# Dot products kept as three components through the edge loop of a graph convolution, and folded per node in the last stage

## The reference, cut to what matters

```
w = edge_query @ tp_weight                      # 224 weights an edge
out0 = w0 * es * sh_s                           # 64
out1 = (w1 * es)[:, :, None] * sh_v             # 64 x 3
out2 = 2**-0.5 * (w2a*sh_s) * ev + 0.5 * w2b * cross(ev, sh_v)      # 32 x 3
out3 = 3**-0.5 * w3 * sum(ev * sh_v, axis=-1)   # 32, the dot products
agg  = segment_sum([out0, out1, out2, out3], edge_dst)              # 384 a node
scal = [a0, a3] @ lin2_w0 / 96**0.5;  vec = [a1, a2] @ lin2_w1 / 96**0.5
x = layernorm(x + skip + [scal, vec] / 10)
```

## Time and profile before

| what | value |
|---|---|
| median of three runs | 7921.6 us (7917.41 to 7922.39) |
| profiled execution, its own time | 7914.6 us |
| its span, first to last instruction | 7912.8 us |
| busy over the span: PE, DVE, ACT, POOL | 89%, 96%, 66%, 68% |
| conv_edges, first L1345 to last L1280 | 5429.6 to 7837.2 us |
| conv_output, from there to the end | 75.6 us |

### The profile page before, as it was taken

How to read it: one execution, slowest core, us unless ns; L and a number is a source line. 1 busy time by engine, 2 the same in 40 slices (tenths; PEclk the granted TensorE clock), 3 DMA queues, 4 the chain that set the end, 5 groups by cost and what they waited for, 6 DMA issues and landing times. The chain is left out here.

```text
span 7912.8 us, 199441 instructions
## 1 busy us (share of the span) xinstructions
PE 7045.1 (89%) x48227; PEld 5905.9 (75%) x48227; DVE 7568.2 (96%) x18615; ACT 5259.2 (66%) x18286; POOL 5348.1 (68%) x5500
## 2 busy tenths in 40 slices
PE   6999999999999999999999859998888888888888
PEld 4888888888888888888888848875555555555556
DVE  4999999999999999999999889976999999999999
ACT  2666666666666666666666634435788788788786
POOL 2777777777777777777777436634777777777773
PEclk5999999999999999999999979977999999999999
DMA  3444444434434344343434337732333333333332
GB/s 105 107 109 109 106 107 106 107 106 106 107 105 107 106 107 106 106 108 105 107 106 107 89 128 260 257 117 69 94 93 91 90 91 90 91 91 90 91 91 59
DMA packets 815660, 856.41 MB, mean 108 GB/s; under 512 B 413920, under 2 KB 623200, under 8 KB 815072
## 3 DMA queue, kind: packets, MB, share of 16 engines
q0 software_dynamic: 241920, 413.20, 21.8%
q1 hardware_dynamic: 573088, 438.30, 18.1%
q10 hardware_dynamic: 576, 4.01, 0.1%
HBM read 706.51 MB, written 148.44 MB: 108 GB/s over the span
## 5 line engine op out<-in xcount | busy, mean ns | idle before, releaser
L1243 POOL DMA_INDIRECT agg<-tab_conv,ce_idx x1808 | 1708.7, 945 | 841.3 <-issue 621.8
L471 POOL DMA_INDIRECT ae_gdst<-tab_dst,ae_idx x1616 | 1683.9, 1042 | 528.0 <-issue 528.0
L468 POOL DMA_INDIRECT ae_gsrc<-tab_src,ae_idx x1616 | 1538.5, 952 | 674.4 <-issue 523.9
L1333 PE MATMUL psum<-ce_prod,ce_plain 128*128 128x384 f32 x3616 | 1539.7, 507 | 302.5 <-ACT ce_prod L1318 302.1
L1318 ACT ACTIVATE ce_prod<-ce_raw,ce_y 128x64 f32<-128x64 f32 x5424 | 1464.8, 333 | 0.0
L1316 ACT ACTIVATE ce_prod<-ce_raw,ce_y 128x160 f32<-128x160 f32 x1808 | 753.2, 417 | 488.8 <-DVE ce_raw L1264 488.8
L1335 PEld LDWEIGHTS psum<-ce_prod,ce_plain 128*128 128x128 f32 x3616 | 687.6, 190 | 479.6 <-issue 1.5
L713 ACT ACTIVATE ae_second_t<-psum 128x512 f32<-128x512 f32 x1212 | 732.2, 604 | 462.0 <-PE psum L623 456.1
L1333 PEld LDWEIGHTS psum<-ce_prod,ce_plain 128*128 128x128 f32 x3616 | 546.9, 191 | 449.5 <-DVE ce_plain L1294 276.2
L631 PE MATMUL psum<-pack_sb,ae_first_t 128*128 128x200 f32 x3232 | 850.1, 345 | 2.2 <-ACT ae_first_t L709 2.0
L641 PE MATMUL psum<-pack_sb,ae_second_t 128*128 128x96 f32 x3232 | 665.1, 288 | 129.1 <-ACT ae_second_t L713 126.7
(11 more groups left out here) (216 smaller groups left out, 19066.1 us busy)
## 6 DMA issues: line engine op xcount, KB each, us to landing
ag_val<-h_dram SPq DMA_DIRECT2D x452, 320.0 KB, 4.0
h_dram<-ae_hout SPq DMA_DIRECT2D x404, 320.0 KB
agg<-in_query SPq DMA_DIRECT2D x452, 128.0 KB
ae_rin<-in_rin SPq DMA_DIRECT2D x404, 128.0 KB
agg<-tab_conv,ce_idx POOLq DMA_INDIRECT x1808
ae_gsrc<-tab_src,ae_idx POOLq DMA_INDIRECT x1616
ae_gdst<-tab_dst,ae_idx POOLq DMA_INDIRECT x1616
ce_idx<-in_eidx SPq DMA_DIRECT2D x452, 4.0 KB
```

Source lines behind the costliest of these rows:

```text
L468: pool.indirect_dma_start(gsrc[t.slot4][:, k, :], None, g["tab_src"], bass.IndirectOffsetOnAxis(ap=idx[t.slot4][:, k:k + 1], axis=0))\
L471: pool.indirect_dma_start(gdst[t.slot4][:, k, :], None, g["tab_dst"], bass.IndirectOffsetOnAxis(ap=idx[t.slot4][:, 4 + k:5 + k], axis=0))\
L1243: pool.indirect_dma_start(node[t.slot8][:, k, :], None, g["tab_conv"], bass.IndirectOffsetOnAxis(ap=idx[t.slot8][:, k:k + 1], axis=0))\
L1333: pe.matmul(b_a[t.slot], plain[t.slot4][:, k, :], prod[t.slot][:, k, 96:480], start=(k == 0), stop=False, skip_group_check=True)
```

## The change

- `prod` is 544 columns wide for each k instead of 480, the block's sum `b_a` 448 instead of 384, `agg1` 448 a node. The three components of a dot product stay apart: columns 352 to 448 of a node hold 3 x 32.
- DVE: the sum over components (L1287) and the product of 128 elements (L1306) are gone. In L1287's place stands one product of 384 elements, weights times `diag`, straight into `prod`. L1303 is now the last of the step and raises `prod_done`. L1280 adds 448 columns.
- PE: L1333 has 448 columns. ACT writes the same sizes to other columns.
- conv_output: 14 additions at the head of DVE's stream fold the three components into one; PE's transposes wait for the fold of their seven blocks. One of the three products has 160 output columns (it had 64) and comes first.
- The table `yy` of the attention layer is allocated in an inner scope.

```diff
+AGG = 448
-        prod = [sb(f"prod{u}", [P, 4, 480]) for u in range(2)]
+        prod = [sb(f"prod{u}", [P, 4, V3 + AGG]) for u in range(2)]
...
-        b_a = [banks[4 + u][:, 0:384] for u in range(2)]
+        b_a = [banks[4 + u][:, 0:AGG] for u in range(2)]
...
-                        wait(dve, dot_done, t.n)
+                        wait(dve, prod_done, t.n)
                         dve.tensor_tensor(both[:, :, :, :, :].rearrange("p k d x c -> p k d (x c)"),
...
-                        dve.tensor_reduce(dot[:, :, :], diag[:, :, :, :].rearrange("p k x c -> p k c x"), AX, ALU.add).then_inc(dot_done, 1)
+                        wait(dve, summed, t.n - 1)
+                        dve.tensor_tensor(comps(prod[t.slot][:, :, 448:544]), b_w[t.slot][:, :, 192:WW].unsqueeze(2).to_broadcast(three),
+                                          diag, ALU.mult)
...
                         dve.wait_ge(cross_done, t.n + 1)
-                        wait(dve, summed, t.n - 1)
-                        dve.tensor_tensor(out[:, :, 192:480].rearrange("p k (x c) -> p k x c", x=3)[:, :, :, CS:96],
-                                          bank[:, :, 160:192].unsqueeze(2).to_broadcast(three), cross[:, :, :, :], ALU.mult)
-                        dve.wait_ge(dot_done, t.n + 1)
-                        dve.tensor_tensor(out[:, :, 160:192], bank[:, :, 192:WW], dot[:, :, :], ALU.mult).then_inc(prod_done, 1)
+                        dve.tensor_tensor(out[:, :, 160:448].rearrange("p k (x c) -> p k x c", x=3)[:, :, :, CS:96],
+                                          bank[:, :, 160:192].unsqueeze(2).to_broadcast(three), cross[:, :, :, :], ALU.mult)\
+                            .then_inc(prod_done, 1)
...
-                            pe.matmul(b_a[t.slot], plain[t.slot4][:, k, :], prod[t.slot][:, k, 96:480], start=(k == 0), stop=False,
+                            pe.matmul(b_a[t.slot], plain[t.slot4][:, k, :], prod[t.slot][:, k, 96:544], start=(k == 0), stop=False,
...
+                for c, (a, z) in enumerate(SEVENS):
+                    dot = agg[:, a:z, 352:384]
+                    dve.tensor_tensor(dot, dot, agg[:, a:z, 384:416], ALU.add).then_inc(halved, 1)
+                    dve.wait_ge(halved, c + 1)
+                    dve.tensor_tensor(dot, dot, agg[:, a:z, 416:448], ALU.add).then_inc(folded, 1)
...
+                        pe.wait_ge(folded, b // 7 + 1)
...
-                        pe.matmul(b_o[b % 4][:, 0:96], feat[b % 4][:, 0, :], w("l2a"), start=True, stop=False, skip_group_check=True)
-                        pe.matmul(b_o[b % 4][:, 64:128], feat[b % 4][:, 1, :], w("l2b"), start=False, stop=False, skip_group_check=True)
-                        pe.matmul(b_o[b % 4][:, 96:160], feat[b % 4][:, 2, :], w("l2c"), start=False, stop=True, skip_group_check=True)\
+                        pe.matmul(b_o[b % 4][:, 0:C], feat[b % 4][:, 2, :], w("l2c"), start=True, stop=False, skip_group_check=True)
+                        pe.matmul(b_o[b % 4][:, 0:96], feat[b % 4][:, 0, :], w("l2a"), start=False, stop=False, skip_group_check=True)
+                        pe.matmul(b_o[b % 4][:, 64:128], feat[b % 4][:, 1, :], w("l2b"), start=False, stop=True, skip_group_check=True)\
```

More of the change, by code:

```diff
@@ L54 @@
     ("ts1", 64, 128), ("tv1", 96, 192), ("tp", 128, 224),
[1 row of a table removed]
+    ("l2a", 128, 96), ("l2b", 128, 64), ("l2c", 128, C),
 ]
@@ L113, in gnn @@
         step_b = top.enter_context(nc.sbuf_tensor("step_b", [P, STEPS], I32))
-        yy = top.enter_context(nc.sbuf_tensor("yy", [P, 4 * SUPER], F32))
         psum = top.enter_context(nc.psum_tensor("psum", [P, 8, 512], F32))
         banks = [psum[:, i, :] for i in range(8)]
-        g = dict(psum=psum, pack=pack, nodes=nodes, block128=block128, step_s=step_s, step_b=step_b, banks=banks, yy=yy,
+        g = dict(psum=psum, pack=pack, nodes=nodes, block128=block128, step_s=step_s, step_b=step_b, banks=banks,
                  tab_src=tab_src, tab_dst=tab_dst, tab_conv=tab_conv, h_dram=h_dram, io=io)
@@ L123, in gnn @@
         g["w"] = w
-        attention_input(nc, g)
         with ExitStack() as mid:
@@ L128, in gnn @@
             with ExitStack() as upper:
+                g["yy"] = upper.enter_context(nc.sbuf_tensor("yy", [P, 4 * SUPER], F32))
+                attention_input(nc, g)
                 g["alpha"] = upper.enter_context(nc.sbuf_tensor("alpha", [P, SCANT, H], F32))
@@ L134, in gnn @@
                 attention_aggregate(nc, g)
-            g["agg1"] = mid.enter_context(nc.sbuf_tensor("agg1", [P, BLOCKS, 384], F32))
+            g["agg1"] = mid.enter_context(nc.sbuf_tensor("agg1", [P, BLOCKS, AGG], F32))
             attention_output(nc, g)
@@ L1208, in conv_edges @@
         diag, plus = both[:, :, 0, :, :], both[:, :, 1, :, :]
-        cross, dot = sb("cross", [P, 4, 3, CV]), sb("dot", [P, 4, CV])
+        cross = sb("cross", [P, 4, 3, CV])
         loaded, gathered = ([sem(f"{x}{u}") for u in range(8)] for x in ("loaded", "gathered"))
-        may_gather, iota_done, raw_done, outer_done, cross_done, plain_done, turned_y, dot_done, prod_done = (sem(x) for x in (
-            "may_gather", "iota_done", "raw_done", "outer_done", "cross_done", "plain_done", "turned_y", "dot_done", "prod_done"))
+        may_gather, iota_done, raw_done, outer_done, cross_done, plain_done, turned_y, prod_done = (sem(x) for x in (
+            "may_gather", "iota_done", "raw_done", "outer_done", "cross_done", "plain_done", "turned_y", "prod_done"))
         scaled, weights, summed, added = (sem(x) for x in ("scaled", "weights", "summed", "added"))
         b_w = [psum[:, 2 * u:2 * u + 2, :].rearrange("p b (k c) -> p (b k) c", k=2)[:, :, 0:WW] for u in range(2)]
-        b_a = [banks[4 + u][:, 0:384] for u in range(2)]
+        b_a = [banks[4 + u][:, 0:AGG] for u in range(2)]
         minus = banks[6][:, 0:384].rearrange("p (k x c) -> p k x c", k=4, x=3)
@@ L1317, in body @@
                         for x in range(3):
-                            ins = act.activation(prod[t.slot][:, k, 192 + 96 * x:256 + 96 * x], raw[t.slot][:, k, 160:WW], ACT.Identity,
+                            ins = act.activation(prod[t.slot][:, k, 160 + 96 * x:224 + 96 * x], raw[t.slot][:, k, 160:WW], ACT.Identity,
                                                  scale=y[t.slot8][:, k, x + 1:x + 2])
@@ L1332, in body @@
                         for k in range(4):
-                            pe.matmul(b_a[t.slot], plain[t.slot4][:, k, :], prod[t.slot][:, k, 96:480], start=(k == 0), stop=False,
+                            pe.matmul(b_a[t.slot], plain[t.slot4][:, k, :], prod[t.slot][:, k, 96:544], start=(k == 0), stop=False,
                                       skip_group_check=True)
-                            ins = pe.matmul(b_a[t.slot][:, 96:384].rearrange("p (x c) -> p x c", x=3)[:, :, CS:96],
+                            ins = pe.matmul(b_a[t.slot][:, 64:352].rearrange("p (x c) -> p x c", x=3)[:, :, CS:96],
                                             plain[t.slot4][:, k, :], prod[t.slot][:, k, 0:96].rearrange("p (x c) -> p x c", x=3),
@@ L1364, in conv_output @@
         turned, kept, mapped, added, rooted, stored = (sem(x) for x in ("turned", "kept", "mapped", "added", "rooted", "stored"))
+        halved, folded = sem("halved"), sem("folded")
         phase = [sem("phase0"), sem("phase1")]
@@ L1513, in lay_pack @@
     lin_s, lin_v = L1["lin2_w0"], L1["lin2_w1"]
-    W["l2a"][0:96, 0:64], W["l2a"][96:128, 64:96] = lin_s, lin_v[0:32]
-    W["l2b"][0:64, 0:32], W["l2b"][64:128, 32:64] = lin_v[32:96], lin_v[0:64]
-    W["l2c"][0:32, 0:32], W["l2c"][32:128, 32:64] = lin_v[64:96], lin_v
+    W["l2a"][0:64, 0:64], W["l2a"][64:128, 64:96] = lin_s[0:64], lin_v[0:64]
+    W["l2b"][0:32, 0:32], W["l2b"][32:128, 32:64] = lin_v[64:96], lin_v
+    W["l2c"][0:96, 128:160], W["l2c"][96:128, 0:64] = lin_v, lin_s[64:96]
     out = np.zeros((P, PACKW), np.float32)
```

## The result

The changed kernel takes 7954.1 us (median of 6 runs, 7951.5 to 7956.8), the kernel before 7917.9 us in the same comparison (6 runs, 7913.1 to 7922.4). The ratio is 1.0046, 95% interval 1.0033 to 1.0059. It is slower by 36 us; forecast were 58, and the range 7945 to 8012 holds it.

The account below looks back on a forecast made before the run. The prediction took DVE, at 5.296 us a step, as the bound, with the ring of engines 0.20 us in two steps behind. 54 us in conv_edges plus 4 in conv_output made 58, forecast 7980 us, range 7945 to 8012.

Parts of the forecast that it names:

- the ring of two steps: conv_edges: chain through DVE, ACT and PE from L1261 to L1261 two steps later, growing from 10.39 to 10.83 us.
- The sign that was expected: conv_edges: L1261 on DVE waits for PE's L1345 in nearly every step, 0.2 to 0.35 us.
- `prod_done` comes earlier, but PE's wait is for ACT, so nothing is gained there: conv_edges, PE's wait before the sums: the earlier semaphore gains nothing; ACT's end to PE's start stays 0.20 us.
- PE's end to L1262: conv_edges: joint from the end of PE's weights to DVE's first instruction of a step (L1261 before), 0.11 us.
- What returns every eight steps: conv_edges: 56 turns of the eight-step loop, up to 17 us on top, counted only at the upper end.
- the ring's forecast of 54: conv_edges: a step of 5.415 us against 5.296, 0.12 us more in each of 452 steps, 54 us.
- conv_output: Folds on DVE and the product with 160 columns: 0.8 + 0.8 + 2.5, about 4 us more, bounds 0 and 10.
- the ring at 0.45 and 0.14: conv_edges, upper bound: columns at 0.45 us and PE to DVE at 0.14, given as 61 us.
- L1264's 0.65 us instead of 0.55: conv_edges, DVE: 0.65 us in the full stretch, where starts are stamped early, 0.55 where DVE stood idle.
- The 1.19 us taken from the idle rows: conv_edges: from L1261's start on an idle DVE, through L1264's end, to ACT's start, 1.19 us.
- DVE is the bound and gains in full: Rival, conv_edges: DVE's saving of 0.16 us a step shows in full, about 7854 us; chance 0.10.
- Half the price a column: Rival, conv_edges: added columns cost PE 0.22 us a step, half of the forecast's, about 7930 us; chance 0.04.

Follow-up runs that it names:

- weights first: The changed kernel with PE's edge-loop body turned round, weights of step m+1 before sums of step m-1: 7843.9 us, ratio to the kernel before 0.9902.
- before_448: The kernel before with PE's large product of the sums (L1333) 448 columns wide, 64 of them unused: 7972.2 us, ratio 1.0067.
- after_512: The changed kernel with PE's large product of the sums 512 columns wide, 64 of them unused: 8052.2 us, ratio to the kernel before 1.0169.
- before_weights_first: The kernel before with PE's edge-loop body turned round, weights ahead of sums: 7917.0 us against 7920.0, ratio 0.9995.
- after_384: The changed kernel with sums 384 columns wide again on PE and in DVE's addition: 11,872 us on the slow chip, 7858.3 us run again elsewhere.

## Why the prediction came out as it did

The mechanism was right: in the timeline DVE waits for PE at L1262, the ring of two steps sets the pace, DVE's own step is 5.14 as forecast (5.129 with weights first), PE's work is 5.07 (6404.26 to 6409.33) where 5.08 stood, and cutting the ring returns everything. The size was off by 22 us of 58. The sign that was expected, a wait of DVE in nearly every step, came in every other one: behind a long step the next runs at DVE's own 5.14. By the prediction's own steps:

- **"`prod_done` comes earlier, but PE's wait is for ACT, so nothing is gained there"** was wrong. The profile names ACT, because its end is the last event, 0.05 us behind L1306's; but with its 0.25 us against ACT's 0.10, `prod_done` was what released PE. The change moved it to 0.23 us ahead of ACT's end (L1305 ends at 6414.59, ACT at 6414.82), and the joint shrank from 0.20 to 0.10. In the whole edge loop this is 0.05 x 452 = 23 us less. In before_448 it did not move, and the joint stayed at 0.20. That its step is the forecast's 5.415 to the last digit is luck all the same: two other terms of the forecast were off there, the shorter way from PE to L1262 and what returns every eight steps (0.26 us), and they cancel.
- **PE's end to L1262**: 0.11 forecast; 6408.30 + 1.03 to 6409.37 is 0.04. That is another 0.035 a step, 16 us less.
- **What returns every eight steps**, left at zero in the middle of the forecast: pairs of steps take 10.65 us, but 10.76 and 10.91 in two of four, 0.37 us for each eight steps. The loop turns 54 times, not 56: 20 us more. More than half of the measured 34.8 us is this; the kernel before showed nothing of it in its steps as DVE was ahead. The forecast had it only in its upper bound (17 us), and put all of it down to the turns. Together the three are -23 - 16 + 20 = -19, and the ring's forecast of 54 becomes 35.
- **conv_output**: 4 forecast, 1.9 measured from L1262's last start. The folds took 0.72 us for each group, PE's first blocks ran beside them, and DVE caught up within two blocks.

```profile
7875.24 0.39 DVE L1409 TENSOR_TENSOR agg<-agg 128x224 f32<-128x224 f32 x1 [0.33 <-PEq L1226]
7875.66 0.39 DVE L1411 TENSOR_TENSOR agg<-agg 128x224 f32<-128x224 f32 x1
...
7880.34 0.55 DVE L1416 TENSOR_TENSOR nodes<-nodes,psum 128x160 f32<-128x160 f32 x2
7881.85 0.32 DVE L1416 TENSOR_TENSOR nodes<-nodes,psum 128x160 f32<-128x160 f32 x1 [0.96 <-PE psum L1448]
```

So the forecast lies 22 us from the time because three errors of 16 to 23 us partly cancel; the ring of two steps is what the experiments confirm. In the upper bound, the ring at 0.45 and 0.14 gives 63 us and not 61, which changes nothing here. One reading of the prediction is doubtful: L1264's 0.65 us instead of 0.55 is not the mark of a DVE that is never idle, for with weights first the kernel before has a full DVE and 0.55 (at 6515.55 us). The 1.19 us taken from the idle rows held: 6409.37 to 6410.56.

The rivals: "DVE is the bound and gains in full" is the kernel with weights first, at 7844 where 7854 was given; it needed a change in PE's order that was not part of this one. The Trainium skill (Perfetto Trace Analysis, "Identifying the Most-Contended Engine") would optimise the engine of highest occupancy first; here DVE's work fell by 3% and the kernel got slower, and the rule gave its gain only once the ring was cut. "Half the price a column" is refuted by PE's time for sums and weights, 4.64 us before and 5.07 after, and by after_512, where 64 more columns cost 98 us: 0.217 a step, half of PE's 0.43.

## What to carry to other kernels

An engine that is 100% busy can be one of two bounds only 2% apart; before giving its work to another engine, add up the loop of waits through all engines over as many steps as the order of the other engine's stream spans. Once that loop is the bound, work added to an engine in it shows in full in the loop, however idle that engine is; moving what starts the next step ahead of it in the same stream (here the weights before the sums, 110 us) is the first thing to try. A wait's last event is not always its releaser: compare the distances in a kernel where one of them moves.

## What the runs showed of the hardware

- From an event to the first product behind several waits in PE's stream took 0.05 us where it was the last of two waits (L1305's end at 6509.02 to 6509.07; the same 0.05 in before_weights_first, where PE had been idle for 0.6 us), 0.10 as second of four, 0.25 as third of four; the third place cost as much with `prod_done` in it as with `scaled`. The Trainium skill (Perfetto Trace Analysis, "Identifying Dependency Chains") notes that extra instructions may be put ahead of one that waits for several engines. No run shows which instruction takes the 0.15 us, and the number of waits still to come does not explain it, as fewer stand behind the third than behind the second.
- A loop body twice as long cost 58 us, with two long pairs of steps at each turn and 1.46 MB of instructions loaded where 0.34 were.
- Eight steps cost 0.37 us more than four pairs of 10.65 once DVE was no longer ahead, and nothing while it was. About 0.2 of it goes with the turn of the loop, 0.15 does not.
- One chip ran the five kernels timed on it, the one before included, in 11,870 to 11,949 us instead of 7918 or so. Its DMA moved 59 to 68 GB/s through most of the attention's edge loop where 105 to 110 are usual. In the convolution's edge loop of after_384 there it moved 67 GB/s (89 in the changed kernel elsewhere), the granted clock was 0.88 instead of 1.00 and the mean step 7.2 us; at that pace none of these differences shows. What made the chip slow is open.
